# Linear attention with 64 heads: the product with the running state from unmasked queries, 16 matmuls of 144 columns in place of 64 of 36

## The chip, the cores and the metric

The kernel runs on one core of a Trainium2 chip. The metric is the device time of one execution in microseconds, the median of several runs. The core has a matrix engine (TensorE; PE in the profile, and PEld for its weight loads), a vector engine (VectorE, DVE), an activation engine (ScalarE, ACT), a general engine (GpSimd, POOL), and SyncE (SP), which here issues nearly all DMAs. Each engine runs its own list of instructions in order, and they meet at semaphores.

## The reference

The input `x` is 4 sequences of 2048 tokens of 512 features. One layer is computed: layer norm, then a causal linear attention with 64 heads of 8 features and a linear layer in fp8 values, side by side, and all of it added to `x`.

```python
xn = _layernorm(x)
q, k, v = heads(xn @ Wq.T + bq), heads(xn @ Wk.T + bk), heads(xn @ Wv.T + bv)
be = exp(beta)
q = softmax(be * q, axis=-1)          # over the 8 features of a head
k = softmax(be * k, axis=-1)
kv = cumsum(einsum('zsD,zsd->zsDd', k, v), axis=1)   # an 8x8 state per head, token by token
kn = cumsum(k, axis=1)
num = einsum('zsD,zsDd->zsd', q, kv)
den = sum(q * kn, axis=-1, keepdims=True)
attn = (num / den) @ Wo.T + bo
ffn = fp8(xn / in_scale) * in_scale @ (w_fp8 * w_scale).T + bias
out = x + attn + ffn
```

## The kernel before, in words

**Tiling.** A step takes 32 tokens (`TOK`) of each of the 4 sequences, so 128 partitions, and there are 64 steps. Heads go in groups of `J` = 4: 16 groups (`G`), each of 4 x 8 = 32 features. A value row has `VW` = 9 columns, 8 features and a one (scaled) that carries the denominator. The causal sum is split: inside a step by masked scores ("intra"), and for all earlier tokens by a running state ("inter").

**One step on TensorE** (`body(i)` of the tensor block), with the lines of the profile. Projections are 12 matmuls of 512 fp16 columns each (high and low halves of both operands). The order in a body is: keys of step i (L877 to L881 into `k_ps`); first half of the scores of step i-1 (L904) and of its state product (L921, 32x32 tiles, into `a_ps`); transposes of step i-2 (L947); queries of step i (`q_ps`); second half of scores and state; the fp8 layer of step i-2 (L979, 4 matmuls) and its output projection (L888 to L892); the **inter product** of step i-1 (L1001) into `a_ps`; values of step i (L877 to L881 into `vo_ps`); the **intra product** of step i-1 (L1020), added onto the inter product in `a_ps`. Scores, state, inter and intra are fp32. Both L1001 and L1020 use 128x32 tiles: all 128 rows of the array, and one of its four bands of 32 columns.

The inter product takes, for each of 16 groups and each of 4 heads j, the 32 tokens' queries with all but head j set to zero (`q_heads`), against a state of 4 sequences x 9 = 36 columns (`st_seqs`), and writes 32 partitions of `a_ps`, those of head j. The rows of the operands are (sequence, head in group, feature), so `st_seqs` is block-diagonal over sequences, and the zeros of `q_heads` pick the head:

```python
for g in range(G):
    for j in range(J):
        mm(a_ps[TOK * j:TOK * (j + 1), a_col(g):a_col(g) + GW],
           q_heads[:, t.parity, g, j, :], st_seqs[:, t.parity, g, :, :],
           start=(g % (G // 2) == 0), stop=False, skip_group_check=True)
```

**Around it.** VectorE masks the state product as it reads it from `a_ps` (`mask_state`, L652, two halves per step) so that only the blocks of equal heads stay. The inter product writes over the same banks, so it waits for the second of them (`masked_ready`). Then `add_state` sums the four heads' columns into `st_step` (L661) and adds that to `st_run` (L666). ScalarE spreads `st_run` over the sequences into `st_seqs` (L529, four activations of 144 columns), which the inter product of the next body reads. ScalarE also makes `q_heads` from the transposed queries `qT` (L520, four activations of 512 columns), which the scores read too, and `k_pairs` (L505).

**What sets the order.** The engines' lists are written out by hand, and each waits on semaphores only. TensorE has one list with all 62 bodies from step 2 on written out (the branch on `any_low`; the other side of it is a loop that doesn't run with these inputs). The other engines run a loop of 4 bodies. VectorE's order in a body is: `normalise_attention` of i-2, `normalise` and `quantise` of x, shift of the keys (L641, L645), masks of scores (L672), `mask_state` 0, the low half of the attention output (L749), key sums (L700 to L712), shift of the queries, masks of scores, transpose of the queries (L769), `mask_state` 1, `output` (L721), `add_state`, statistics, and in every second body `variances`, then `scale_values` (L728).

## Time and profile before

| | |
|---|---|
| runs | 1307.56, 1312.95, 1318.35 us; median 1312.95 us |
| the profiled execution | 1305.86 us; span 1304.1 us |
| mean granted clock of TensorE | 0.977 of full |
| TensorE busy | 1195.1 us, 92% of the span |
| VectorE busy | 1025.0 us, 79% |
| ScalarE busy | 661.0 us, 51% |
| GpSimd busy | 321.7 us, 25% |
| a step in the even middle part | 18.1 and 18.4 us in turn |

The busy shares are means over the span. The last row is read from the timeline, as the distance of one inter product's start to the next. Of a matmul the profile shows start and a modelled end; the ends overlap the next starts, so what a group of matmuls takes is read from its first start to the start of the group behind it. An fp32 matmul that isn't a transpose stands in the profile as two weight loads and two matmuls.

### The profile page before, as it was taken

Reading aid. Unit: us, or ns where it says so; the run is one execution under the profiler, and the core shown is the slowest. Engines: PE = TensorE matmul, PEld = TensorE weight load, DVE = VectorE, ACT = ScalarE, POOL = GpSimd, SP = SyncE. Lnnn points to the kernel's source line nnn. Section 1 sums busy time; section 2 is a strip of 40 time slices with the busy share of each in tenths; the row PEclk is TensorE's granted clock in tenths of the full one; section 3 lists DMA queues with packets and bytes.
Section 4 is the critical chain, followed back from the end, with each engine's and each line's share of the span. In section 5 each row is a group of like instructions: output and inputs, shape, how many; then the busy total and the mean of one; then the engine's idle time right before and its main releaser. Section 6 shows DMA issues by size and latency. Waiting matters only on the chain.

```text
span 1304.1 us, 72799 instructions
## 1 busy us (share of the span) xinstructions
PE 1195.1 (92%) x32226; PEld 700.8 (54%) x32226; DVE 1025.0 (79%) x2031; ACT 661.0 (51%) x1177; POOL 321.7 (25%) x590
## 2 busy tenths in 40 slices
PE   1469898889898999999999999999999999999996
PEld 1335454555455555555555555555555555555553
DVE  3668686777687788888888888888888888888873
ACT  0555454444454555555555555555555555555541
POOL 3132221221222222222222222222222222222210
PEclk8689999999999999999999999999999999999998
DMA  9024343333233334344444343334333343333321
GB/s 229 16 66 73 72 76 70 72 75 68 73 69 86 75 76 88 79 84 81 88 89 82 80 86 90 83 83 79 89 87 81 85 81 92 84 82 80 70 69 44
DMA packets 156531, 105.41 MB, mean 81 GB/s; under 512 B 111969, under 2 KB 128481, under 8 KB 156257
## 3 DMA queue, kind: packets, MB, share of 16 engines
q1 hardware_dynamic: 155536, 99.76, 35.2%
q8 instruction: 256, 4.19, 1.4%
q10 hardware_dynamic: 720, 1.31, 0.4%
q14 instruction: 19, 0.15, 0.0%
HBM read 40.20 MB, written 16.78 MB: 44 GB/s over the span
## 4 chain that ended last, share of the span: by engine, by line
PE 89%; issue 6%; DVE 2%; DMA 1%; POOL 0%; ACT 0%; SPq 0%; POOLq 0%; DVEq 0%; ACTq 0%
PE s_ps L904 10%; PE a_ps L921 7%; PE a_ps L1001 6%; PE a_ps L1020 6%; PE k_ps L877 5%; PE vo_ps L979 5%; PE vo_ps L877 5%; PE k_ps L881 4%; PE k_ps L879 4%; PE vo_ps L888 4%; PE vo_ps L890 4%; PE vo_ps L879 4%; PE vo_ps L892 4%; PE vo_ps L881 4%; PE q_ps L879 4%
## 5 line engine op out<-in xcount | busy, mean ns | idle before, releaser
L520 ACT ACTIVATE q_heads<-qT,cst 128x512 f32<-128x512 f32 x256 | 164.0, 712 | 88.1 <-DVE qT L769 88.1
L406 POOL TENSOR_TENSOR y_sum<-y,y_magic 128x512 f32<-128x512 f32 x64 | 81.5, 1273 | 433.2 <-DVE y_magic L627 433.2
L505 ACT ACTIVATE k_pairs<-kT,cst 128x512 f32<-128x512 f32 x128 | 85.4, 714 | 166.7 <-DVE kT L712 166.7
L672 DVE TENSOR_TENSOR att<-s_ps,cst 128x512 f32<-128x512 f32 x256 | 163.7, 681 | 0.4 <-PE s_ps L904 0.4
L399 POOL TENSOR_TENSOR x_split<-xn,x_split 128x512 f16<-128x512 f32 x64 | 74.1, 1158 | 318.5 <-ACT x_split L461 311.5
L904 PE MATMUL s_ps<-q_heads,k_pairs 64*64 64x128 f32 x4096 | 141.5, 276 | 0.6 <-DVE att L672 0.6
L904 PEld LDWEIGHTS s_ps<-q_heads,k_pairs 64*64 64x64 f32 x4096 | 110.6, 133 | 54.5 <-issue 54.5
L461 ACT ACTIVATE x_split<-xn 128x512 f16<-128x512 f32 x64 | 40.3, 630 | 158.6 <-DVE xn L616 158.6
L877 PE MATMUL k_ps<-w_hi,xT 128*128 128x512 f16 x256 | 100.2, 392 | 21.8 <-DMA xT<-x_split 12.1
L879 PE MATMUL vo_ps<-w_lo,xT 128*128 128x512 f16 x256 | 97.8, 382 | 4.2 <-issue 4.2
L881 PE MATMUL k_ps<-w_hi,xT 128*128 128x512 f16 x256 | 99.4, 388 | 2.3 <-issue 2.3
L1001 PEld LDWEIGHTS a_ps<-st_seqs,q_heads 128*32 128x32 f32 x8192 | 78.5, 109 | 42.0 <-issue 41.8
L881 PE MATMUL vo_ps<-w_hi,xT 128*128 128x512 f16 x256 | 97.8, 382 | 3.3 <-issue 3.3
L1020 PEld LDWEIGHTS a_ps<-v_groups,att 128*32 128x32 f32 x8192 | 77.9, 108 | 40.6 <-issue 40.5
L1020 PE MATMUL a_ps<-v_groups,att 128*32 128x36 f32 x8192 | 86.5, 200 | 14.3 <-issue 14.2
L879 PE MATMUL k_ps<-w_lo,xT 128*128 128x512 f16 x256 | 99.4, 388 | 0.0
L890 PE MATMUL vo_ps<-w_lo,ah 128*128 128x512 f16 x260 | 99.0, 381 | 0.0
L888 PE MATMUL vo_ps<-w_hi,ah 128*128 128x512 f16 x260 | 99.0, 381 | 0.0
L892 PE MATMUL vo_ps<-w_hi,al 128*128 128x512 f16 x260 | 99.0, 381 | 0.0
L1001 PE MATMUL a_ps<-st_seqs,q_heads 128*32 128x36 f32 x8192 | 85.2, 201 | 14.5 <-issue 13.3
L877 PE MATMUL vo_ps<-w_hi,xT 128*128 128x512 f16 x256 | 98.2, 384 | 0.0
L921 PE MATMUL a_ps<-vp,k_e 32*32 32x36 f32 x8064 | 97.1, 196 | 0.0
(137 smaller groups left out, 2363.8 us busy)
## 6 DMA issues: line engine op xcount, KB each, us to landing
v_groups<-vp SPq DMA_DIRECT2D x512, 36.0 KB, 3.0
x_in<-L_attn_x SPq DMA_DIRECT2D x64, 256.0 KB
x_res<-L_attn_x SPq DMA_DIRECT2D x64, 256.0 KB
out<-o_sb SPq DMA_DIRECT2D x64, 256.0 KB
w_own<-L_attn_Wk SPq DMA_DIRECT2D x1, 1024.0 KB, 13.3
w_own<-L_attn_Wq SPq DMA_DIRECT2D x1, 1024.0 KB, 15.3
w_own<-L_attn_Wv SPq DMA_DIRECT2D x1, 1024.0 KB, 17.2
att<-L_ffn_weight_fp SPq DMA_DIRECT2D x1, 1024.0 KB, 18.8
```

What stands on the lines that cost most here:

```text
L520: last = sc.activation(q_heads[:, i.parity, :, j, :], qT[:, :, :], ACT.Copy, scale=head_mask[:, j:j + 1])
L672: v.tensor_tensor(att[:, c % 2, 4 * (c // 2):4 * (c // 2) + 4, :, :] .rearrange("p g j s -> p (g j) s"), s_ps[:, DM * (c % 2):DM * (c % 2 ...
L877: mm(bank[:, :], xT[:, t.parity, 0, c, :], w_hi[:, m, c, :], start=(c == 0 and not seeded), stop=False, skip_group_check=seeded)
L879: mm(bank[:, :], xT[:, t.parity, 0, c, :], w_lo[:, m, c, :], start=False, stop=False, skip_group_check=seeded)
L881: last = mm(bank[:, :], xT[:, t.parity, 1, c, :], w_hi[:, m, c, :], start=False, stop=(c == KC - 1), skip_group_check=seeded)
L888: mm(vo_ps[:, :], ah[:, j, :], w_hi[:, MO, j, :], start=(j == 0 and not rest), stop=False, skip_group_check=rest)
L890: mm(vo_ps[:, :], ah[:, j, :], w_lo[:, MO, j, :], start=False, stop=False, skip_group_check=rest)
L892: last = mm(vo_ps[:, :], al[:, j, :], w_hi[:, MO, j, :], start=False, stop=(j == J - 1), skip_group_check=rest)
L904: last = mm(s_ps[SP * TOK * gp:SP * TOK * (gp + 1), DM * n + P * q:DM * n + P * (q + 1)], k_pairs[rows, t.parity, g, :, :].rearrange("p c ...
L921: last = mm(a_ps[rows, col:col + J * VW], k_e[rows, t.parity, TOK * g:TOK * (g + 1)], vp[rows, t.parity, v_head(g):v_head(g) + J, :], star ...
L1001: mm(a_ps[TOK * j:TOK * (j + 1), a_col(g):a_col(g) + GW], q_heads[:, t.parity, g, j, :], st_seqs[:, t.parity, g, :, :], start=(g % (G // 2 ...
L1020: last = mm(groups[TOK * j:TOK * (j + 1), n], att[:, n, q, j, :], v_groups[:, t.parity, :, n, q, j, :], start=False, stop=True, skip_group ...
```

## The change

The inter product takes the unmasked queries `qT` of a group, 32 columns, once, and a state that is block-diagonal over heads as well as sequences: 4 heads x 4 sequences x 9 = 144 columns. It writes the same 4608 columns in all per step, as 16 matmuls of 144 instead of 64 of 36. A band of 32 partitions of `a_ps` no longer holds a head of the group but a group in its quarter (u); the intra product, `wo_sorted` and `bv_sorted` follow that order. The state in `st_run` keeps its masked 4 x 9 columns per group (576 in all), so the reduction over heads goes, the addition is of 576 columns, and each of the four activations into `st_seqs` is of 576 columns. `qT` has two buffers, with other waits. To make room, `lo_abs` and `k_pairs` lie in weight buffers that are read only during setup. Lines behind the first edits shift: in the changed kernel L1001 is L999, L1020 is L1018, L904 is L900, L921 is L917, L666 is L665, L529 is L530.

```diff
-        lo_abs = sb("lo_abs", [P, KC * DM], F16)
+        lo_abs = w_own[2][:, 0:KC // 2, :].rearrange("p c d -> p (c d)").bitcast(F16)
-        qT = sb("qT", [P, G, TOK])
+        qT = sb("qT", [P, 2, G, TOK])
-        k_pairs = sb("k_pairs", [P, 2, G, SP, TOK])
+        k_pairs = w_own[1][:, :, :].rearrange("p (n c) (g s) -> p n (c g) s", n=2, s=TOK)\
+            .rearrange("p n (g c) s -> p n g c s", c=SP)
-        st_step = sb("st_step", [P, G, VW])
-        st_run = sb("st_run", [P, G, VW])
-        st_seqs = sb("st_seqs", [P, 2, G, SEQS, VW])
+        st_run = sb("st_run", [P, G, J, VW])
+        st_seqs = sb("st_seqs", [P, 2, G, J, SEQS, VW])
...
# scalar engine
                     if i.after(2):
-                        act.wait_ge(a_done, (i - 1).n)
+                        act.wait_ge(scores_done, (i - 1).n * 2)
                     for j in range(J):
-                        last = sc.activation(q_heads[:, i.parity, :, j, :], qT[:, :, :],
+                        last = sc.activation(q_heads[:, i.parity, :, j, :], qT[:, i.parity, :, :],
                                              ACT.Copy, scale=head_mask[:, j:j + 1])
...
-                        last = sc.activation(st_seqs[:, i.parity, :, b, :], st_run[:, :, :],
+                        last = sc.activation(st_seqs[:, i.parity, :, :, b, :].rearrange("p g j w -> p (g j) w"),
+                                             st_run[:, :, :, :].rearrange("p g j w -> p (g j) w"),
                                              ACT.Copy, scale=seq_mask[:, b:b + 1])
...
# vector engine
-            link(v.memset(st_run[:, :, :], 0.0))
-            link(v.memset(st_seqs[:, 0, :, :, :], 0.0))
+            link(v.memset(st_run[:, :, :, :], 0.0))
+            link(v.memset(st_seqs[:, 0].rearrange("p g j b w -> p (g j b w)"), 0.0))
...
                 dve.wait_ge(masked_ready, (t + 1).n * 2)
-                v.tensor_reduce(st_step[:, :, :], st_masked[:, :, :, :].rearrange("p g j w -> p g w j"),
-                                AX.X, ALU.add).then_inc(ststep_ready, 1)
-                dve.wait_ge(ststep_ready, (t + 1).n)
                 if t.after(1):
                     dve.wait_ge(stseqs_ready, t.n)
-                v.tensor_tensor(st_run[:, :, :], st_run[:, :, :], st_step[:, :, :], ALU.add)\
+                v.tensor_tensor(st_run[:, :, :, :], st_run[:, :, :, :], st_masked[:, :, :, :], ALU.add)\
                     .then_inc(strun_ready, 1)
...
-                    if i.after(1):
-                        dve.wait_ge(qheads_ready, i.n)
-                    v.transpose(qT[:, :, :].rearrange("p g s -> p (g s)"), q_e[:, :]).then_inc(qT_ready, 1)
+                    if i.after(2):
+                        dve.wait_ge(qheads_ready, (i - 1).n)
+                        dve.wait_ge(a_done, (i - 1).n)
+                    v.transpose(qT[:, i.parity].rearrange("p g s -> p (g s)"), q_e[:, :]).then_inc(qT_ready, 1)
...
# tensor engine
-                    pe.wait_ge(qheads_ready, (t + 1).n)
+                    pe.wait_ge(qT_ready, (t + 1).n)
...
-                    for g in range(G):
-                        for j in range(J):
-                            mm(a_ps[TOK * j:TOK * (j + 1), a_col(g):a_col(g) + GW],
-                               q_heads[:, t.parity, g, j, :], st_seqs[:, t.parity, g, :, :],
-                               start=(g % (G // 2) == 0), stop=False, skip_group_check=True)
+                    for n in range(2):
+                        for gp in range(GP):
+                            for u in range(J):
+                                g = G // 2 * n + GP * u + gp
+                                mm(a_rows[TOK * u:TOK * (u + 1), n, gp, :], qT[:, t.parity, g, :],
+                                   st_seqs[:, t.parity, g].rearrange("p j b w -> p (j b w)"),
+                                   start=(gp == 0), stop=False, skip_group_check=True)
...
-                    for q in range(G // GP):
-                        groups = a_ps[:, a_col(GP * q):a_col(GP * q) + GP * GW]\
-                            .rearrange("p (g n w) -> p n g w", g=GP, w=SP * VW)
+                    for h in range(2):
                         for n in range(SEQS // SP):
                             for j in range(J):
-                                last = mm(groups[TOK * j:TOK * (j + 1), n], att[:, n, q, j, :],
-                                          v_groups[:, t.parity, :, n, q, j, :], start=False, stop=True,
-                                          skip_group_check=True)
+                                cols = slice(GW * j + SP * VW * n, GW * j + SP * VW * (n + 1))
+                                for u in range(J):
+                                    last = mm(a_rows[TOK * u:TOK * (u + 1), h, :, cols],
+                                              att[:, n, J * h + u, j, :],
+                                              v_groups[:, t.parity, :, n, J * h + u, j, :], start=False, stop=True,
+                                              skip_group_check=True)
```

Two places in the engines' lists, as the programs were built. First TensorE, around the inter product of one body (`a_ps` is the result, `vo_ps` the bank of the projections). Before:

```order
L892 MATMUL vo_ps<-w_hi,al 128x512
L1001 MATMUL a_ps<-st_seqs,q_heads 32x36 [waits stseqs_ready,masked_ready,qheads_ready]
L1001 MATMUL a_ps<-st_seqs,q_heads 32x36 x63
L877 MATMUL vo_ps<-w_hi,xT 128x512 [waits o_ready]
L879 MATMUL vo_ps<-w_lo,xT 128x512
```

And now:

```order
L888 MATMUL vo_ps<-w_hi,al 128x512
L999 MATMUL a_ps<-st_seqs,qT 32x144 [waits stseqs_ready,masked_ready,qT_ready]
L999 MATMUL a_ps<-st_seqs,qT 32x144 x15
L873 MATMUL vo_ps<-w_hi,xT 128x512 [waits o_ready]
L875 MATMUL vo_ps<-w_lo,xT 128x512
```

Nothing changes its place; 48 fp32 matmuls, which are 192 instructions, are gone from each body. A body had 1008 weight loads and matmuls and 13 instructions that only wait or signal, 1021 in all; it has 829 now, and the list from its start to the end of the last step has 65,294 before and 53,006 now. Then VectorE, from the transpose of the queries to the statistics. Before:

```order
L769 STREAM_TRANSPOSE qT<-q_e 128x512 [waits qheads_ready,qe_ready]
L652 TENSOR_TENSOR st_masked<-a_ps,cst 128x288 [waits state_done]
L721 SCALAR_TENSOR_TENSOR o_sb<-vo_ps,out_dn,x_res 128x512 [waits stored1,r_loaded1,o_done]
L660 REGISTER_ALU
L661 TENSOR_REDUCE st_step<-st_masked 128x144 [waits masked_ready]
L666 TENSOR_TENSOR st_run<-st_run,st_step 128x144 [waits stseqs_ready,ststep_ready]
```

And now:

```order
L769 STREAM_TRANSPOSE qT<-q_e 128x512 [waits a_done,qheads_ready,qe_ready]
L654 TENSOR_TENSOR st_masked<-a_ps,cst 128x288 [waits state_done]
L720 SCALAR_TENSOR_TENSOR o_sb<-vo_ps,out_dn,x_res 128x512 [waits stored1,r_loaded1,o_done]
L662 REGISTER_ALU
L665 TENSOR_TENSOR st_run<-st_run,st_masked 128x576 [waits stseqs_ready,masked_ready]
```

One instruction fewer, and it stands behind `mask_state` 1 and `output`; ahead of them only a wait is added.

## Rows read from the trace of the kernel before

**Rows 1.** The page: busy times, and TensorE's instruction fetch (packets, MB, share).

```profile
PE 1195.1 (92%) x32226; PEld 700.8 (54%) x32226; DVE 1025.0 (79%) x2031; ACT 661.0 (51%) x1177; POOL 321.7 (25%) x590
q8 instruction: 256, 4.19, 1.4%
```

**Rows 2.** Windows, from:to length, busy (instructions) by engine, granted clock, DMA.

```profile
195.00:217.30 22.30, 20.05 (x504) 10.97 (x504) 15.60 (x33) 9.88 (x19) 5.94 (x16) 0.92 0.31 66
600.00:800.00 200.00, 198.81 (x5543) 117.11 (x5541) 171.02 (x340) 109.68 (x196) 54.85 (x105) 1.00 0.41 85
```

**Rows 3.** Timeline of TensorE, one step: start, length, what, [idle before].

```profile
706.22 1.30 PE L1001 MATMUL a_ps<-st_seqs,q_heads 128*32 128x36 f32 x128 [0.27 <-issue]
707.46 0.39 PE L877 MATMUL vo_ps<-w_hi,xT 128*128 128x512 f16 x1
...
714.09 1.10 PE L904 MATMUL s_ps<-q_heads,k_pairs 64*64 64x128 f32 x32
...
715.12 0.76 PE L921 MATMUL a_ps<-vp,k_e 32*32 32x36 f32 x64
...
715.81 0.66 PE L947 MATMUL t_ps<-cst,a_n 128*128 128x128 f32 x4
```

**Rows 4.** Timeline of VectorE and TensorE: from a state mask to the next inter product.

```profile
723.81 0.42 DVE L652 TENSOR_TENSOR st_masked<-a_ps,cst 128x288 f32<-128x288 f32 x1
...
732.37 0.69 DVE L641 TENSOR_REDUCE k_max<-k_ps 128x64 f32<-128x512 f32 x1 [0.55 <-PE k_ps L881]
...
742.25 0.42 DVE L652 TENSOR_TENSOR st_masked<-a_ps,cst 128x288 f32<-128x288 f32 x1
...
742.77 0.43 PE L1001 MATMUL a_ps<-st_seqs,q_heads 128*32 128x36 f32 x28 [0.25 <-issue]
```

**Rows 5.** Waits of TensorE put down to issue: total us, times, longest.

```profile
PE a_ps L1020 <- issue: 14.2, 10, 2.2
PE a_ps L1001 <- issue: 13.3, 29, 2.6
PE k_ps L877 <- issue: 5.3, 5, 2.3
PE vo_ps L879 <- issue: 4.2, 3, 2.1
PE vo_ps L881 <- issue: 3.3, 3, 1.6
PE k_ps L881 <- issue: 2.3, 3, 1.1
```

**Rows 6.** Timeline of TensorE at two of these stalls.

```profile
199.00 0.39 PE L879 MATMUL vo_ps<-w_lo,xT 128*128 128x512 f16 x1 [2.11 <-issue]
...
200.04 0.63 PE L881 MATMUL vo_ps<-w_hi,xT 128*128 128x512 f16 x1
...
371.00 1.30 PE L1020 MATMUL a_ps<-v_groups,att 128*32 128x36 f32 x127
374.27 0.19 PE L1020 MATMUL a_ps<-v_groups,att 128*32 128x36 f32 x1 [1.97 <-issue]
```

**Rows 7.** Groups by line, whole span: xcount, busy us, mean ns, idle before.

```profile
L661 DVE TENSOR_REDUCE st_step<-st_masked 128x144 f32<-128x576 f32 x63 | 75.2, 1193 | 0.0
L666 DVE TENSOR_TENSOR st_run<-st_run,st_step 128x144 f32<-128x144 f32 x63 | 19.4, 308 | 2.2
L672 DVE TENSOR_TENSOR att<-s_ps,cst 128x512 f32<-128x512 f32 x256 | 163.7, 681 | 0.4 <-PE s_ps L904 0.4
L520 ACT ACTIVATE q_heads<-qT,cst 128x512 f32<-128x512 f32 x256 | 164.0, 712 | 88.1 <-DVE qT L769 88.1
L529 ACT ACTIVATE st_seqs<-st_run,cst 128x144 f32<-128x144 f32 x252 | 84.7, 411 | 7.0 <-DVE st_run L666 4.0
```

**Rows 8.** Waits, as rows 5: VectorE and ScalarE behind the values.

```profile
ACT vo_ps L476 <- DVE vp L728: 97.2, 63, 5.7
...
DVE vp L728 <- PE vo_ps L881: 63.5, 63, 4.7
```

More of the change, by code:

```diff
@@ L224, in build @@
         a_view = a_halves[:, :, 0:G // 2 * GW]
+        a_rows = a_view.rearrange("p n (l r) -> p n l r", l=GP)
         setup_banks = [b[:, n * DM:(n + 1) * DM] for b, n in
@@ L260, in build @@
         scores_done, att_ready = sem("scores_done"), sem("att_ready")
-        state_done, masked_ready, ststep_ready = sem("state_done"), sem("masked_ready"), sem("ststep_ready")
+        state_done, masked_ready = sem("state_done"), sem("masked_ready")
         strun_ready, stseqs_ready = sem("strun_ready"), sem("stseqs_ready")
@@ L437, in _ @@
                     .then_inc(bias_ready, 1)
-            gp.tensor_tensor(bv_sorted.rearrange("p (j g d) -> p j g d", j=J, d=DH),
-                             bias[:, MV, :].rearrange("p (g j d) -> p j g d", j=J, d=DH),
-                             w_scale_up[:, MV:MV + 1, None, None].to_broadcast([P, J, G, DH]), ALU.mult)\
+            gp.tensor_tensor(bv_sorted.rearrange("p (u h r) -> p u h r", u=J, h=2),
+                             bias[:, MV, :].rearrange("p (h u r) -> p u h r", u=J, h=2),
+                             w_scale_up[:, MV:MV + 1, None, None].to_broadcast([P, J, 2, DM // J // 2]), ALU.mult)\
                 .then_inc(bias_ready, 1)
@@ L543, in late_weights @@
                 for oc in range(KC):
-                    last = sc.activation(wo_sorted[:, oc, :].rearrange("p (j g d) -> p j g d", j=J, d=DH),
-                                         w_nat[MO][:, oc, :].rearrange("p (g j d) -> p j g d", j=J, d=DH),
+                    last = sc.activation(wo_sorted[:, oc, :].rearrange("p (u h r) -> p u h r", u=J, h=2),
+                                         w_nat[MO][:, oc, :].rearrange("p (h u r) -> p u h r", u=J, h=2),
                                          ACT.Copy)
@@ L551, in late_weights @@
                 act.wait_ge(wl_ready, chunks - KC)
-                sc.activation(lo_abs[:, :], w_lo[:, MF, :, :].rearrange("p c d -> p (c d)"), ACT.Abs,
+                sc.activation(lo_abs, w_lo[:, MF, :, :].rearrange("p c d -> p (c d)"), ACT.Abs,
                               accum_out=lo_sum[:, :]).then_inc(lo_summed, 1)
@@ L864, in _ @@
             transpose = nc.tensor.transpose
-            def a_col(g):
-                return DM * (g // (G // 2)) + GW * (g % (G // 2))
             def v_head(g):
```

## The prediction, made before the changed kernel ran

> **What bounds the kernel now.** The page comes first: TensorE is busy for 92% of the span, VectorE for 79%, the others far less [rows 1]. In the even middle part it is 198.8 of 200 us [rows 2], so there a step is as long as what TensorE has to do, or nearly. The timeline says how nearly. The inter product starts at 742.77, and the second `mask_state` ends at 742.25 + 0.42 = 742.67; TensorE stood idle for 0.25 us and was let go by VectorE, though the row says "issue" [rows 4]. The body before it starts its inter product 0.10 us behind the mask too. So the middle part is a ring of both engines: keys done, then VectorE's list from `k_max` (732.37) to the mask's end (742.67), 10.3 us, then inter, values, intra and keys on TensorE. TensorE alone would take about 18.07 us a step, which is the distance in the last full steps; the ring takes 18.1 and 18.4 in turn. Whatever shortens the inter product shortens both.
>
> The early part is slower, 20 to 23 us a step between 195 and 400 us, and the waits of TensorE say by what: idle time that no engine released, at six lines [rows 5]. Of the 13.3 us at L1001, 7.0 are three stalls of 2.1 to 2.6 us and the rest are the small waits for the mask; of the 5.3 at k_ps L877, 0.8 lies in setup. This leaves 14.2 + 7.0 + 4.5 + 4.2 + 3.3 + 2.3 = 35.5 us. Two of them are in [rows 6]: one after the first value matmul, one before the last record of the intra product. Counted in the program's list, they are all at one place: 194 or 195 instructions behind a multiple of 256, in all of the 16 that I placed, the one at 1288 us too. The list has 65,294 instructions, 255.05 times 256, and the fetch queue moved 256 packets, 4.19 MB, so 16 KB or 256 instructions each [rows 1]. So these are fetches of instructions that come late. A body is 1021 instructions, 3 less than 4 blocks, so the boundary creeps through the body by 3 a step. It hurts while a whole block is consumed in the two dense products, where 256 instructions take 1.24 us (706.22 to 707.46 [rows 3]), and not later on. At the stall of 374.27 the block had begun with the group at 371.00: 3.3 us from block to block. With 3.45 us as the least time of a block, a count along the list gives 36.4 us of stalls against the 35.5 seen, in the same steps.
>
> The Trainium skill, Runtime: NRT & Kernel Launch, section Instruction fetch mechanics, has the 256-instruction blocks too, and says that crossing a boundary is mostly hidden, since instructions are dispatched more slowly than they are filled. By that sentence fewer instructions would be worth nothing here; the trace disagrees, with 35.5 us.
>
> **The change, part by part.**
>
> *The inter product itself.* From start to the next group's start, L1001 takes 1.24 us for 128 matmul records of 36 columns, L921 0.69 us for 64: 8.6 ns each and 0.14 us once. L904 takes 1.03 us for 32 records of 128 columns: less 0.14, 27.8 ns each [rows 3]. Four run beside each other, so one tile spends 4 x 8.6 = 34.4 ns on 36 columns and 111 on 128: 0.83 ns a column. 144 columns cost 124 ns a tile, 31.1 ns a record, and 32 records with the 0.14 make 1.13 us instead of 1.24. **This is 0.11 us a step, 64 times: 6.7 us.** The columns stay the same; only the share per instruction goes. Bounds: 0.96 us, if four tiles stream without a gap and nothing is paid once (0.28 less, -18 us); from above the overlap of tiles with 128 rows and long streams isn't in any row. L904's tiles have 64 rows. Tiles of 128 rows overlap well at 36 columns, with the same 4608 columns in 1.24 us. I take the middle value since L904 is the nearest in columns.
>
> The Trainium skill, TensorE: Matmul & The Clock Gate, section Part 3: Packing small matmuls, says that a weight load overlaps a running matmul only where the row group differs. All four tiles here have all rows, so it speaks against long streams; at 36 columns the trace disagrees, with 8.6 ns a record. The same section gives a speedup of 2.38 for three column tiles, about 0.8 of ideal; as an estimate from it the inter product would take 1.39 us, and the sum would have 10 us more in place of 6.7 less.
>
> *Instruction fetch.* A body has 192 instructions fewer, 829, which is 3 blocks and 61. The boundary jumps by 61 a step now instead of creeping by 3, and the inter product is 64 instructions instead of 256. Only a block that is nearly all intra product is consumed too fast. The same count along the new list, with 3.45 us a block, finds it in every fourth or fifth body: bodies 8, 12, 17, 21 (0.6, 1.8, 1.9, 0.7 us), 29, 33, 38, 42 (0.4, 1.6, 2.1, 0.9), 50, 54, 59, 63 (0.4, 1.6, 2.1, 0.9), and once more at the end (1.9): 17 us. It hardly depends on where the first boundary lies (15 to 18 us for any). **35.5 - 17 = 18.5 us less.** Bounds: all 35.5 gone, or none.
>
> *The clock.* After four of the eleven stalls of 1.9 us and more, six to eight matmuls came 0.43 us apart instead of 0.215 (199.66 to 202.60 is one place [rows 6]), and the granted clock of that body is 0.92 against 1.00 in the middle [rows 2]: 1.2 GHz instead of 2.4. That was 5.6 us. With four or five such stalls left, 2 to 3 us stay: **3 us less**.
>
> *VectorE.* `add_state` was 1.19 + 0.31 us; one addition of 576 columns, by the 512 of L672 at 0.68, is 0.75 [rows 7]. The 0.75 us saved lie behind `output`, outside the ring's 10.3 us, in front of a wait for the values. Costed at nothing; should the addition be dearer, the cover is VectorE's wait for the values, 63.5 us in 63 bodies, 1.0 us each [rows 8]. Without the cover each 0.1 us costs 6 us. The added wait of the transpose of the queries is for an intra product one body back: nothing.
>
> *ScalarE.* Four activations of 576 columns: by L520 at 0.71 (512) and L529 at 0.41 (144) [rows 7], some 0.75 each, 3.0 us instead of 1.4 with their overlap. Next in its queue is the seed of `vo_ps`, for which it waited 1.5 us a body [rows 8]; that takes nearly all of the added 1.5 us, and the fp8 layer on TensorE needs the seed only after scores, transposes and the query projection. `st_seqs` itself is read by the inter product a body later, about 14 us. Nothing; uncovered it would be 1.5 us a step, 96 us.
>
> *The rest.* The intra product has the same matmuls in another order: nothing. The larger memsets (2304 and 576 columns) are on VectorE at the start, ahead of a wait for the scalars' DMA: nothing, and 3 us once if that wait were shorter. The aliased buffers are free before their first new use.
>
> Sum: 6.7 + 18.5 + 3 = 28 us off the profiled execution's 1305.9, 1278. The median of the runs lies 7 above that execution, which is inside their own spread of 11; I take half: **1281 us**.
>
> **The rivals.**
>
> 1. *The fetch gain doesn't come*: the stalls stay, because late fetches follow something else in the first 500 us (the DMA load, say) and not the density of instructions. For it: they come in the first 500 us only. Against: the place modulo 256, and the one at 1288. Then 6.7 us: about 1302 to 1306. This is also how it would go by the sentence of the skill on fetching.
> 2. *The tiles overlap less*, 3.2 of them at a time: 32 x 124 / 3.2 + 0.14 us = 1.38 us for the inter product, 0.14 more a step than before. Then 9 us more where 6.7 less were counted: 1297, just faster by over 1%; 1290 to 1300 with milder forms. The section of the skill on packing would have it so. For it: L904's four tiles have half the rows. Against: the 36-column tiles.
> 3. *Slower: the bands serialise.* If a weight load or a stream of 144 columns waits for the one before, whatever the band, 32 records cost 32 x 124 ns = 4.0 us and the 0.14 once, 2.9 us more a step: 1281 + 6.7 + 185 = 1473 us. It turns the change to a loss once the inter product takes over 1.24 + 21.5 / 64 = 1.58 us, when fewer than 2.8 tiles run at a time. For it: no row shows it excluded at this length. Against: 36-column tiles of the same shape overlap almost fully.
> 4. *More*: all stalls go, and the product is at 0.96 us: 18 + 35 + 5.6 = 59 us less, 1250 to 1255.
>
> **How the numbers follow.** A difference under about 1%, 13 us, can't be told from none here. The forecast has 0.57 (its own range 1272 to 1292), rival 1 0.13, rival 2 0.18, rival 3 and weaker forms of it 0.06, rival 4 0.06. Faster by over 1%, below 1300: the forecast, rival 4 and nearly all of rival 2 are 0.79; same 0.15; slower 0.06. The range leaves out rival 3, most of rival 4 and the upper part of rival 1: 1260 to 1303.
>
> **What would show it.** In the changed profile: L999 to the next L873 in 1.1 to 1.2 us; the fetch queue with 208 packets (53,006 instructions); issue stalls of 15 to 18 us in all, in single bodies over the whole span and not in a run of bodies, mostly near L1018, and the early steps as short as the late ones; the middle steps 18.0 and 18.3 us, with the inter product still 0.1 us behind the mask. Wrong would be: an inter group over 1.5 us; more or longer stalls than 20 us; or the inter product waiting for `st_seqs`, which would mean that ScalarE's longer work isn't covered.

## The result, and the profile after

| | before | changed |
|---|---|---|
| runs, us | median 1310.48 (1307.56 to 1318.35) | median 1251.41 (1250.03 to 1252.23) |
| ratio, 95% interval | | 0.954 [0.949, 0.959] |
| the profiled execution | 1305.86 us, span 1304.1 | 1250.03 us, span 1248.2 |
| mean granted clock | 0.977 | 0.982 |
| first to last inter product | 1188.8 us | 1137.7 us |

The medians (four runs of each) are 59 us apart and the profiled executions 55.8, where the prediction's sum had 28. The forecast was 1281 us; the result lies below the predicted range of 1260 to 1303. The page of the changed kernel, for [rows 1]:

```profile
PE 1174.9 (94%) x26082; PEld 679.2 (54%) x26082; DVE 977.9 (78%) x1968; ACT 744.9 (60%) x1177; POOL 321.6 (26%) x590
q8 instruction: 209, 3.42, 1.2%
```

The fetch queue moved 209 packets where 208 were counted, 47 fewer than before. VectorE lost 47 us of work and ScalarE gained 84, and neither is seen in the time. The two windows of [rows 2], in the changed kernel:

```profile
195.00:217.30 22.30, 22.30 (x505) 13.00 (x495) 18.16 (x36) 13.11 (x21) 3.71 (x3) 1.00 0.37 90
600.00:800.00 200.00, 199.16 (x4492) 114.78 (x4490) 162.69 (x329) 125.26 (x199) 52.49 (x93) 1.00 0.38 84
```

The middle is as it was. The early window was 20.05 of 22.30 us busy at a granted clock of 0.92; now TensorE is busy without a gap at 1.00. One step's timeline of TensorE, for [rows 3], and the state mask of VectorE ahead of it, for [rows 4]:

```profile
712.25 1.19 PE L999 MATMUL a_ps<-st_seqs,qT 128*32 128x144 f32 x32
713.37 0.39 PE L873 MATMUL vo_ps<-w_hi,xT 128*128 128x512 f16 x1
...
716.07 1.31 PE L1018 MATMUL a_ps<-v_groups,att 128*32 128x36 f32 x128
```

```profile
711.73 0.42 DVE L654 TENSOR_TENSOR st_masked<-a_ps,cst 128x288 f32<-128x288 f32 x1
```

The inter product takes 1.12 us (712.25 to 713.37) and still starts 0.10 us behind the mask's end (712.15): the ring is there, with steps of 18.00 and 18.28 us in place of 18.11 and 18.40. The first nine rows of TensorE's waits, for [rows 5] and [rows 6]:

```profile
PE q_ps L1039 <- DMA w_own<-L_attn_Wk: 17.2, 1, 17.2
PE q_ps L1039 <- DVE w_lo L805: 15.0, 1, 15.0
PE k_ps L873 <- DMA xT<-x_split: 12.3, 1, 12.3
PE a_ps L999 <- issue: 5.8, 24, 0.3
PE k_ps L873 <- ACT k_ps L568: 3.8, 1, 3.8
PE k_ps L1050 <- DVE w_lo L805: 3.5, 1, 3.5
PE s_ps L1039 <- DVE w_lo L805: 3.2, 2, 2.1
PE t_ps L943 <- DVE a_n L690: 1.8, 2, 1.5
PE k_ps L873 <- issue: 0.8, 1, 0.8
```

Of the six lines of "issue" in [rows 5], the only one that is left besides the 0.8 us of setup is the inter product's, at most 0.3 us each time: the small waits for the mask. **Not one stall of instruction fetch is left.** The groups and the wait that answer to [rows 7] and [rows 8]:

```profile
L530 ACT ACTIVATE st_seqs<-st_run,cst 128x576 f32<-128x576 f32 x252 | 181.5, 797 | 0.5 <-DVE st_run L665 0.5
...
L665 DVE TENSOR_TENSOR st_run<-st_run,st_masked 128x576 f32<-128x576 f32 x63 | 47.1, 748 | 0.0
```

```profile
DVE vp L727 <- PE vo_ps L877: 86.3, 63, 2.4
```

The addition is 0.748 us (0.75 was estimated), an activation 0.80 (0.75), and VectorE's wait for the values grew from 63.5 to 86.3 us: that is where its saved work went.

**Where the 55.8 us between the profiled executions come from.** From the first inter product to the last, 51.1 us: 7.6 from 63 inter products 0.12 us shorter, 33.6 from the stalls by the profile's idle times, 4.3 from matmuls at 1.2 GHz behind them, and 5.6 that this leaves. Most of the 5.6 is a way of counting: a stall's idle time begins at the modelled end of the last matmul, 0.38 us behind its start, though the next could have come 0.215 behind it, so each of some 25 stalls cost about 0.17 us more than its row says. Behind the last inter product, 4.2 us: one stall of 1.9 and the matmuls at 1.2 GHz after it. Ahead of the first, 0.6.

### The profile page after: what moved, and what is told of

It reads as the page before. It is cut to its first block, busy times and chain, and to the rows that moved or that the text cites. A ratio compares the mean times of both kernels' runs of the same rounds, so it can differ in the third digit from the quotient of the medians.

```text
span 1248.2 us, 60447 instructions
## 1 busy us (share of the span) xinstructions
PE 1174.9 (94%) x26082; PEld 679.2 (54%) x26082; DVE 977.9 (78%) x1968; ACT 744.9 (60%) x1177; POOL 321.6 (26%) x590
## 3 DMA queue, kind: packets, MB, share of 16 engines
q8 instruction: 209, 3.42, 1.2%
## 4 chain that ended last, share of the span: by engine, by line
PE 92%; issue 3%; DVE 2%; DMA 1%; ACT 1%; POOL 1%; SPq 0%; POOLq 0%; DVEq 0%; ACTq 0%
PE s_ps L900 10%; PE a_ps L917 7%; PE a_ps L1018 6%; PE a_ps L999 6%; PE k_ps L873 5%; PE vo_ps L975 5%; PE vo_ps L873 5%; PE k_ps L877 5%; PE k_ps L875 5%; PE vo_ps L884 4%; PE vo_ps L888 4%; PE vo_ps L886 4%; PE vo_ps L877 4%; PE vo_ps L875 4%; PE q_ps L877 4%; PE q_ps L873 4%
## 5 line engine op out<-in xcount | busy, mean ns | idle before, releaser
L506 ACT ACTIVATE w_own<-kT,cst 128x512 f32<-128x512 f32 x128 | 85.5, 715 | 166.7 <-DVE kT L711 166.7
L530 ACT ACTIVATE st_seqs<-st_run,cst 128x576 f32<-128x576 f32 x252 | 181.5, 797 | 0.5 <-DVE st_run L665 0.5
L900 PE MATMUL s_ps<-q_heads,w_own 64*64 64x128 f32 x4096 | 141.3, 275 | 0.6 <-DVE att L671 0.6
L900 PEld LDWEIGHTS s_ps<-q_heads,w_own 64*64 64x64 f32 x4096 | 110.4, 132 | 54.3 <-issue 54.2
L727 DVE TENSOR_TENSOR vp<-vo_ps,vp 128x512 f32<-128x512 f32 x64 | 44.3, 692 | 86.3 <-PE vo_ps L877 86.3
L873 PE MATMUL vo_ps<-w_hi,xT 128*128 128x512 f16 x256 | 97.7, 382 | 0.0
L917 PE MATMUL a_ps<-vp,k_e 32*32 32x36 f32 x8064 | 97.6, 196 | 0.0
L873 PE MATMUL q_ps<-w_hi,xT 128*128 128x512 f16 x256 | 97.0, 379 | 0.0
L875 PE MATMUL q_ps<-w_lo,xT 128*128 128x512 f16 x256 | 97.0, 379 | 0.0
L877 PE MATMUL q_ps<-w_hi,xT 128*128 128x512 f16 x256 | 97.0, 379 | 0.0
```

Source lines behind the costliest of these rows:

```text
L506: last = sc.activation(k_pairs[:, i.parity, :, c, :], kT[:, :, :], ACT.Copy, scale=pair_mask[:, c:c + 1])
L530: last = sc.activation(st_seqs[:, i.parity, :, :, b, :].rearrange("p g j w -> p (g j) w"), st_run[:, :, :, :].rearrange("p g j w -> p (g j ...
L873: mm(bank[:, :], xT[:, t.parity, 0, c, :], w_hi[:, m, c, :], start=(c == 0 and not seeded), stop=False, skip_group_check=seeded)
L875: mm(bank[:, :], xT[:, t.parity, 0, c, :], w_lo[:, m, c, :], start=False, stop=False, skip_group_check=seeded)
L877: last = mm(bank[:, :], xT[:, t.parity, 1, c, :], w_hi[:, m, c, :], start=False, stop=(c == KC - 1), skip_group_check=seeded)
L900: last = mm(s_ps[SP * TOK * gp:SP * TOK * (gp + 1), DM * n + P * q:DM * n + P * (q + 1)], k_pairs[rows, t.parity, g, :, :].rearrange("p c ...
```

## The experiments

In all of them the two transposing DMAs (`xT`, `xq`) are plain copies of the same bytes, so that the projections' operands aren't transposed; beside that each computes what its edit says. Each is a change to one of the two kernels, and all ratios are to the kernel before. Stalls are counted here from start to start: how far apart two neighbouring matmuls are at a block's boundary, less 0.25 us, where 0.3 us or more are left. A block is 256 instructions, "the array" is the part of TensorE that runs the matmuls, and its sequencer is the part that reads the list ahead of it and waits for semaphores. In the expectations theory A is that late fetches made the difference, F that two dense blocks one behind the other are enough for a stall, E and H that a wait which holds the sequencer holds the fetch; B, C and D name other causes.

**1 and 2. Both kernels with plain copies.**

```diff
-                sp.dma_start_transpose(xT[...], x_split[...]).then_inc(x_turned, 16)
+                sp.dma_start(xT[...], x_split[...]).then_inc(x_turned, 16)
```

> The kernel before the change, but each of the two DMA transposes of a body (x_split to xT, xq_rows to xq) is a plain DMA of the same bytes, so the operands aren't transposed. This is the base of the runs that follow, which all have plain copies. Theory A (instruction fetches that start too late for two fast blocks in a row): TensorE's list and the place of the block boundaries stay, so the stalls in bodies 3 to 23 stay too, 25 to 40 us; the step on TensorE stays; 1295 to 1312. Rival D (the fetches are late because the transposes' many small packets crowd the queues): the stalls go here, 1260 to 1270.

> The changed kernel with plain copies in place of the DMA transposes. Theory A (late instruction fetches made the difference): no stalls of over 0.3 us on TensorE, 1247 to 1255, and the distance to the kernel before with copies is 50 to 62 us, as with the transposes. Rival D (the fetches are late because the transposes' many small packets crowd the queues): the distance is about 10 us.

The old kernel: 1312.8 us, ratio to the kernel before 0.999 [0.997, 1.002], with 28 stalls, 43.8 us in all. The changed one: 1248.75 us, 0.954 [0.950, 0.958], with none. The copies change nothing that can be told from none, though the DMA packets are 72,563 in place of 156,531: many small packets are not the cause. The old kernel's steps exceed 18.2 us by 55.7 us in sum, in those steps that a stall hits: a microsecond of stall costs 1.27.

**3. The changed kernel with 64 matmuls of 36 columns again**, from the same unmasked queries and the same state; with the 192 instructions a body back, all else as changed.

```diff
+                            for j in range(0, J, 1):
...
-                                   st_seqs[:, t.parity, g].rearrange("p j b w -> p (j b w)"),
+                                        st_seqs[:, t.parity, g, j:j + 1].rearrange("p j b w -> p (j b w)"),
```

> The changed kernel with plain copies, and the inter product of a body issued as 64 matmuls of 36 columns (unmasked queries, one head's columns of the block-diagonal state each) instead of 16 of 144. All edits on VectorE and ScalarE stay. A body has 1021 instructions for TensorE again, at the same places as before the change. Theory A (late instruction fetches made the difference): the stalls return in bodies 3 to 23, with the low clock behind some; the time is within 5 us of the kernel before with copies. Rival B (the gain comes from the shorter add_state on VectorE, from two buffers of qT, or from the longer streams): the stalls don't return; at most 15 us over the changed kernel with copies.

1308.64 us, 0.998 [0.995, 1.001]. The whole gain is gone, with 26 stalls back, 39.9 us. What the change did on VectorE, ScalarE, in buffers or in the order of the intra product shows no gain of its own beside the stalls.

**4. The same with 32 matmuls of 72 columns** (`range(0, J, 2)`, 64 instructions a body more than the change):

> The changed kernel with plain copies and 32 matmuls of 72 columns for the inter product, 893 instructions a body. Theory E, made from the fetch times of the runs so far: the next block is asked for when TensorE's list is read some 50 instructions behind the boundary; if a semaphore wait stands before that point the request waits too; from the end of that wait to the first instruction of the block it takes 3.4 us. From the mask to the boundary there are here 128 instructions of inter (1.1 us) and at least some of the 24 of the value projection (2.6 us) and only then intra: the block comes in time. Stalls under 2 us in all, 0 to 4 us over the changed kernel with copies (1248.75). Theory A' of the prediction (each block needs 3.45 us by itself): about 15 us over it.

1252.74 us, 0.959 [0.954, 0.963], with two stalls, 2.0 us. So halving the inter product's instructions was enough. One step's row of each, in that order:

```profile
713.28 1.30 PE L1000 MATMUL a_ps<-st_seqs,qT 128*32 128x36 f32 x128 [0.22 <-issue]
```

```profile
711.31 1.21 PE L1000 MATMUL a_ps<-st_seqs,qT 128*32 128x72 f32 x64
712.45 0.39 PE L873 MATMUL vo_ps<-w_hi,xT 128*128 128x512 f16 x1
```

With 72 columns the product takes 1.14 us: nearly all the rate is gained by 72.

**5. The old kernel with its list moved.** 352 waits for a semaphore that has long been reached, which are built as 176 instructions, stand ahead of the first body, which moves every boundary by 176 instructions and leaves the bodies as they are.

```diff
+            for _ in range(352):
+                pe.wait_ge(c_loaded, 16)
```

> The kernel before the change with plain copies, and with 176 instructions that only wait for a semaphore already reached put in at the start of TensorE's list, where it waits for weights. All later instructions move by 176 against the blocks of 256; nothing else changes. Theory A: the boundary lies where no two fast blocks follow each other in bodies 3 to 23; stalls of 2 to 8 us in all, little or no low clock; 28 to 40 us less than the same kernel without the 176. Rival C (the stalls belong to the first 400 us of the program, warm-up or the load of the queues, whatever the place of the boundary): within 5 us of it. Rival B says the same as C.

1298.35 us, 0.989 [0.984, 0.995]. The early stalls are gone (first fifteen steps 18.30 us in the mean, 21.41 without the padding), so the place in the list decides. But 14 stalls, 30.3 us, turned up between 955 and 1282 us, in bodies that had none: my count had forecast 28 to 40 us less, and 12 to 14 came. Where they sit was the way on. TensorE and VectorE at the first of them:

```profile
951.89 1.10 PE L1001 MATMUL a_ps<-st_seqs,q_heads 128*32 128x36 f32 x104 [0.27 <-issue]
955.21 0.40 PE L1001 MATMUL a_ps<-st_seqs,q_heads 128*32 128x36 f32 x24 [2.23 <-issue]
955.55 0.39 PE L877 MATMUL vo_ps<-w_hi,xT 128*128 128x512 f16 x1
955.77 0.54 PE L879 MATMUL vo_ps<-w_lo,xT 128*128 128x512 f16 x1
956.11 0.63 PE L881 MATMUL vo_ps<-w_hi,xT 128*128 128x512 f16 x1
956.54 0.63 PE L877 MATMUL vo_ps<-w_hi,xT 128*128 128x512 f16 x1
```

```profile
951.37 0.42 DVE L652 TENSOR_TENSOR st_masked<-a_ps,cst 128x288 f32<-128x288 f32 x1
```

The array had entered the block at 947.80, 4.1 us ahead of the inter product. The DMA rows have no packet of the instruction queue from 948.0 to 952.8 and one from there to 953.9; its record starts at 952.83:

```profile
q8 instruction: 1, 0.02, 5.6%
```

The mask ended at 951.79, the fetch began 1.04 us later, and the first instruction of the new block ran 2.38 us after that: 3.42 us from the mask's end. The 208 inter instructions of the old block were gone after 0.9 us. In all 13 stalled bodies of this kernel the fetch began 1.03 to 1.74 us behind the mask's end, 0.3 to 5.0 us after the block was entered; in the bodies of 37 to 62 without a stall it began 0.4 to 1.5 us after the block was entered and 2.2 to 3.1 us ahead of the mask's end. That gave the theory: **the sequencer, which asks for the next block, runs ahead of the array, stands at the wait for the mask, and asks only when the mask lets it go.** The trace has rows of the sequencer itself (PEldq) that show it standing there. L998 is its wait for the mask and the queries; the row gives how many there are, the shortest, median and longest in ns, and where they start. In this body:

```profile
L998 PEldq EVENT_SEMAPHORE  x1: 3738/3738/3738, 948.1 to 948.1; - x1
```

It came to the wait at 948.10, 3.8 us ahead of the array, and stood for 3.74 us, until 951.83, 0.04 behind the mask's end; the fetch began 0.99 us later. In the 13 stalled bodies it began 1.0 to 1.7 us behind the end of this row. The rows also show the array slowing down behind the stall: the value matmuls come 0.22, 0.34 and 0.43 us apart, where 0.215 is normal, at a granted clock of 0.52 between 955.77 and 958.50, the 1.2 GHz level.

**6 and 7. The mask ahead of the queries' transpose**, in the old kernel and in the padded one. The mask then ends up to 0.7 us earlier.

```diff
+                if t.exists() and i.exists():
+                    mask_state(t, 1)
                 if i.exists():
                     dve.wait_ge(qe_ready, (i + 1).n)
...
-                if t.exists() and i.exists():
-                    mask_state(t, 1)
```

> The kernel before the change with plain copies and VectorE's second state mask ahead of the transpose of the queries; no padding. Theory E: the stalls of bodies 2 to 6, in or just behind the inter product, go, and without a first stall the ones in intra don't follow; stalls under 8 us in all, 1255 to 1270. Rival F: the stalls of bodies 7 to 23 stay, 25 to 30 us, 1278 to 1300.

> The kernel before the change with plain copies, the 176 instructions at the start, and VectorE's second state mask ahead of the transpose of the queries. TensorE then has no wait at the inter product. Theory E: the stalls of bodies 47 to 62, which came with the wait for the mask, go: stalls under 4 us in all instead of 30, and the step falls to 18.07 us; 1255 to 1264 against 1298 without the reordering. Rival F (two fast blocks in a row, wait or not): only the shorter step, 1287 to 1291.

1285.88 us, 0.985 [0.981, 0.990], and 1282.1 us, 0.981 [0.977, 0.986]. The first lies in theory F's range, 16 us above theory E's; the second misses theory E's 1255 to 1264 by 18 us and theory F's 1287 to 1291 by 5, so neither held as it stood. The stalls stayed: 21 of them, 28.5 us, and 15, 25.1 us. I had taken it that a mask which no longer delays the array no longer delays the sequencer. It does: in the padded kernel the fetch still began 1.01 to 1.30 us behind the mask's end in every stalled body, though that end now lay 0.4 to 0.8 us ahead of the inter product, and the gaps at L1001 were 1.7 to 2.4 us in place of 2.3 to 3.0 (in both without the last body). The stall followed the mask and not the array. The sequencer's wait at L998 was only shorter, 3.01 us in the middle of its 63 times where it was 3.46 in experiment 5. Here it is for experiment 7:

```profile
L998 PEldq EVENT_SEMAPHORE  x63: 51/3011/3150, 110.3 to 1258.9; - x63
```

To take the hold away the mask must be earlier by the whole lead of the sequencer.

**8 and 9. Both masks early.** The second state mask reads the first half again and stands right behind the first, so no inter product waits for it; in the padded old kernel and in the old kernel. The state of the second half of the groups is left out by it; TensorE's list is the same.

```diff
-                dve.wait_ge(state_done, t.n * 2 + n + 1)
+                if n == 0:
+                    dve.wait_ge(state_done, t.n * 2 + 1)
...
-                    a_state[:, n, :].rearrange("p (g j w) -> p g j w", j=J, w=VW),
+                    a_state[:, 0, :].rearrange("p (g j w) -> p g j w", j=J, w=VW),
...
                         mask_state(t, 0)
+                        mask_state(t, 1)
```

> The padded old kernel (176 signals more ahead of the first body), with both state masks made early, right behind the first half of the state product; the second reads the first half again, so the state of the second half of the groups is left out. The inter product then waits for a mask that ended some 8 us before. Theory H (a fetch of instructions is asked for by TensorE's sequencer, and the sequencer stands at the wait for the mask long before the array gets there, so the fetch starts 1.0 to 1.3 us behind the mask's end, and the next block is late where 256 inter instructions follow): the stalls at L1001 in bodies 43 to 62 all go, the last bodies take 17.8 us a step in place of 19.5, one stall of about 2 us stays at the end. From the 1282.1 of the same kernel with the mask only moved ahead of the transpose (stalled steps cost 31.6 us there) this gives 1250 to 1256. Theory F (two dense blocks one behind the other are enough): the stalls stay in those bodies, 1275 to 1283.

> The old kernel with plain copies and the same two early masks (the second reads the first half again, so part of the state is left out). Theory H: the stalls of bodies 0 to 4, where the block before the boundary holds the wait, go (with the mask ahead of the transpose they were 1.6, 2.1, 1.8 and 2.2 us at 116 to 195 us). From body 5 on the boundary lies inside the inter product itself and the fetch can't be ahead there: those stalls stay in part. 1273 to 1284, against 1285.9 with the mask ahead of the transpose. Theory F: as that one, stalls of bodies 1 to 4 included, 1284 to 1289.

The padded one: 1251.47 us, 0.953 [0.949, 0.958], one stall, at the end: inside theory H's 1250 to 1256 and 24 us from F's. The sequencer's wait is gone, all 63 times (51 ns is the shortest such row):

```profile
L998 PEldq EVENT_SEMAPHORE  x63: 51/51/51, 109.7 to 1226.9; - x63
```

At the place of the rows of experiment 5 the inter product is in one piece:

```profile
945.37 1.31 PE L1001 MATMUL a_ps<-st_seqs,q_heads 128*32 128x36 f32 x128
946.62 0.39 PE L877 MATMUL vo_ps<-w_hi,xT 128*128 128x512 f16 x1
```

The old kernel, one run: 1249.83 us, where I had expected 1273 to 1284. The direction was theory H's, the size was not: I had thought that a boundary inside the inter product stalls with or without the hold. It doesn't. **The old kernel, with all its 65,294 TensorE instructions, has one stall left**, and that is 63 us less than experiment 1. The same boundary in both, with the block entered on the first matmuls of the inter product. First experiment 1, TensorE, then VectorE's mask:

```profile
288.22 1.30 PE L1001 MATMUL a_ps<-st_seqs,q_heads 128*32 128x36 f32 x128 [0.25 <-issue]
...
290.75 0.38 PE L877 MATMUL vo_ps<-w_hi,xT 128*128 128x512 f16 x1
291.90 0.39 PE L879 MATMUL vo_ps<-w_lo,xT 128*128 128x512 f16 x1 [0.77 <-issue]
```

```profile
287.70 0.42 DVE L652 TENSOR_TENSOR st_masked<-a_ps,cst 128x288 f32<-128x288 f32 x1
```

and the old kernel with early masks:

```profile
257.05 1.31 PE L1001 MATMUL a_ps<-st_seqs,q_heads 128*32 128x36 f32 x128
...
259.60 0.38 PE L877 MATMUL vo_ps<-w_hi,xT 128*128 128x512 f16 x1
259.81 0.38 PE L879 MATMUL vo_ps<-w_lo,xT 128*128 128x512 f16 x1
```

```profile
249.50 0.81 DVE L653 TENSOR_TENSOR st_masked<-a_ps,cst 128x288 f32<-128x288 f32 x2
```

The sequencer's wait in the first and in the second:

```profile
L998 PEldq EVENT_SEMAPHORE  x1: 3686/3686/3686, 284.5 to 284.5; - x1
```

```profile
L998 PEldq EVENT_SEMAPHORE  x1: 51/51/51, 253.6 to 253.6; - x1
```

In the first it ended at 288.16 and the fetch began at 289.22, 1.0 us after the inter product's start; in the second it ended at 253.68 and the fetch began at 254.76, 2.3 us ahead of the inter product, whose mask had ended at 250.31. So the fetch began 1.06 and 1.08 us behind the wait's end in the two, and only the wait had moved. In bodies 5 to 18, where the boundary lies inside the inter product, this fetch began 1.0 to 1.7 us behind the inter product's start in experiment 1 and 0.1 to 2.3 us ahead of it here. The instruction queue's rows, of 289.1 to 290.3 us in the first kernel and of 254.7 to 255.9 in the second, hold one packet each:

```profile
q8 instruction: 1, 0.02, 7.0%
```

```profile
q8 instruction: 1, 0.02, 4.9%
```

The stall that is left (1.6 us, at 1233.2) is of another kind. It lies in the last body, where no values stand between the inter and the intra product, and the sequencer had not been held; the block before it was entered at 1229.90, its successor's fetch began at 1230.72, and the array had run through the block at 1231.4 and stood until 1233.23. So two dense products one behind the other do stall without any hold, as theory F has it. It happens once, here and in experiments 1 and 3 to 8 (1.4 to 2.1 us), and not in the changed kernel.

**10 and 11. The changed kernel with the mask ahead of the transpose, and with both masks early.** The edits are those of 6 and 8.

> The changed kernel with plain copies, and with VectorE's second state mask ahead of the transpose of the queries instead of behind it. The inter product waits for that mask; it ends 0.6 us earlier. If the ring of VectorE and TensorE sets the step, both steps fall to TensorE's own 17.96 us, 0.04 and 0.32 us less: 9 to 12 us less than the changed kernel with copies. Rival: the queries' transpose and q_heads are late for the next scores, or output (0.75 us, behind the mask on VectorE) holds the values instead: 0 to 4 us less.

> The changed kernel with plain copies and the same two early masks (part of the state is left out). It has no stalls to lose. Against 1239.5 with the second mask ahead of the transpose, where a step took 17.94 us: if that is TensorE's own work, 1237 to 1241; if a ring through the mask is still in it, 1230 to 1236. Late steps of 17.6 us in both cases.

1239.47 us, 0.947 [0.943, 0.951], and 1239.66 us, 0.945 [0.941, 0.950]. The first computes all that experiment 2 does and is **9.3 us faster than it**; no kernel here was clearly faster. Steps are 17.94 and 17.95 us, and TensorE has no idle time in the middle, for [rows 2]:

```profile
600.00:800.00 200.00, 200.00 (x4616) 115.45 (x4616) 163.96 (x333) 127.34 (x202) 53.63 (x99) 1.00 0.29 84
```

So the ring cost 9 us in the changed kernel. A mask earlier still gives nothing more, because there is no stall to lose. With early masks in both, the two kernels are 10.2 us apart (experiments 9 and 11; of 9 there is one run), of which the shorter inter product makes 7.7 and the last stall 1.6: so little of the 59 us belongs to the new product itself.

**12. The changed kernel with the old reduction back on VectorE**, its result unused: 1.19 us more a step.

```diff
+                v.tensor_reduce(st_step[:, :, :], st_masked[:, :, :, :].rearrange("p g j w -> p g w j"),
+                                AX.X, ALU.add)
```

> The changed kernel with plain copies, with the old reduction over heads put back on VectorE ahead of the addition of the state (its result is not used), 1.19 us a body. My account, that add_state stands behind the ring and in front of a wait for the values: VectorE's wait for the values shrinks from 1.4 to about 0.2 us a body; 0 to 4 us over the changed kernel with copies. Rival B (the saving on VectorE counts): 10 to 75 us over it.

1255.71 us, 0.961 [0.957, 0.966], 7 us above experiment 2 and between the two expectations. No stall came. Steps are 18.19 and 18.28 us in place of 18.00 and 18.28: VectorE's wait for the values, first in experiment 2 and then here, is gone in every second body, and in those the reduction lengthens the ring.

```profile
DVE vp L727 <- PE vo_ps L877: 87.1, 63, 2.4
```

```profile
DVE vp L730 <- PE vo_ps L880: 23.8, 33, 1.6
```

The cover is about 1 us a step wide; 1.5 us of old additions fit under it, 1.94 don't.

## Why the prediction was wrong

**The inter product, 6.7 us: right.** 1.12 us was measured against the 1.13 worked out; 64 times 0.12 is 7.7. The tiles of 128 rows overlap at 144 columns as the prediction worked out. By the estimate from the Trainium skill's speedup of 2.38 for three column tiles (TensorE: Matmul & The Clock Gate, section Part 3: Packing small matmuls) it would have taken 1.39 us; the trace does not agree, with 1.12.

**Instruction fetch, 18.5 us: wrong, and this is the step that failed.** All 35.5 us went. The step took 3.45 us as the least time of a block, wherever it lies, and walked along the new list with it, which left 17 us of stalls where none came. The 3.45 itself is near what a late fetch takes: 3.42 us from the mask's end in experiment 5. What failed is that it is not a property of every block but, in all bodies but the last, of a fetch whose asking was held up. The forecast put stalls into the intra product, since a block of it is consumed in 1.24 us. But ahead of the intra product stand the twelve matmuls of the values, 2.6 us, over which the sequencer runs ahead. In the changed kernel one block was entered at 298.29 and left at 299.90, 1.6 us later, without a stall, since its fetch had begun at 297.38:

```profile
298.29 0.38 PE L875 MATMUL vo_ps<-w_lo,xT 128*128 128x512 f16 x1
298.51 0.38 PE L877 MATMUL vo_ps<-w_hi,xT 128*128 128x512 f16 x1
298.81 1.31 PE L1018 MATMUL a_ps<-v_groups,att 128*32 128x36 f32 x128
300.06 0.39 PE L873 MATMUL k_ps<-w_hi,xT 128*128 128x512 f16 x1
```

What the old kernel has and the changed one hasn't is 256 dense instructions right behind a held wait. The hold is still there: with plain copies, in 12 bodies of the changed kernel the fetch begins 1.0 to 1.5 us behind the mask. But now 64 inter instructions and 24 of the values take 3.8 us (712.25 to 716.07), more than the 3.4 that the fetch needs. With 128 (experiment 4) it is nearly always enough too, with 256 (experiment 3) not. The stalls of the old kernel in the intra product and in the keys were followers of the same hold: the fetch at the inter product is late, the next one begins only some 1.5 us (1.3 to 2.1) after the array has entered its block, and the next dense block is late too. With the hold away (experiment 9), they all went. The one of 1.9 us that was forecast for the end did not come either: in experiment 2 the fetch for it began 0.87 us ahead of the last inter product.

The Trainium skill, Runtime: NRT & Kernel Launch, section Instruction fetch mechanics, has the sequencer fetch the next page while it executes the current one. The trace agrees (a packet began 2.3 us ahead of its turn in experiment 9), and adds that a semaphore wait which holds the sequencer holds the fetch too, for the 3.74 us of the row in experiment 5, with 1.0 to 1.7 us from release to packet. The prediction used that section's sentence on dispatch only, and did not ask where the sequencer stands.

**The clock, 3 us: too small,** since it hung on the stalls that were to stay; 4.3 us and most of the 2.3 at the end came.

**VectorE and ScalarE, 0: right.** Experiment 3 has all of their changes and none of the gain. Experiment 12 shows how near the cover's end was. **The rest, 0: right.** The median counted at half its distance from the profiled execution made no difference that matters.

**The ring: right,** in that the inter product stands 0.10 us behind the mask as before. That it could be broken was not in the sum; experiment 10 gave the 9 us that it costs.

**The rivals.** Rival 4, that all stalls go, is what came, at the time it gave (1250 to 1255), with a chance of 0.06. That its time fits is in part luck: its other half, an inter product at 0.96 us, did not come, and the uncounted part of each stall and more of the clock made up for it. The forecast's walk fitted the old list because there the dense inter product stood behind the wait in every body; that it gave 36.4 us for the 35.5 seen was a test on one list only. Rivals 1, 2 and 3 fell: no stall stayed, and the inter product took 1.12 us, not 1.38 or more.

What stays open: in the padded kernels some bodies with the boundary at nearly the same distance ahead of the inter product were held and others not (in experiment 7, 61 and 58 instructions held, 55 to 46 not, 43 held again). The sequencer's rows tell most of them apart. In bodies 37 to 62 of experiments 5 and 7, no body was held whose wait at L998 began 0.37 us or more behind the array's entry into the block (22 bodies), and of the 30 where it began earlier all but three were held. Why those three were not, and what in the chip sets that time, the runs don't show. Nor do they show how close two fetches can be: in the old kernel they were never less than 3.1 us apart, in the changed one two at the end were 0.3 us apart.

## What to carry to other kernels

Stalls "by issue" at places that are a fixed number modulo the block of the list are late instruction fetches, and what made a fetch late here, in all bodies but the last, was a wait that holds the engine's sequencer ahead of a dense run of instructions. The sequencer's own rows (PEldq in the profile) show how long it stands there. Compare the time from the wait's release to the end of the dense run with the 3.4 us of a fetch: either thin out the run behind the wait (fewer, longer instructions, or slow ones between), or let the awaited work end some microseconds earlier, so that the sequencer passes before the array gets there. Before such a model is walked along a new list, move the old list by half a block and see whether the model finds the stalls again.

## What the runs showed of the hardware

- An instruction fetch is one packet of 16 KB that takes about 1 us on the queue; at a stall the first instruction of the new block ran 2.2 to 2.9 us after the packet's start, and where the sequencer had been held the packet started 1.0 to 1.7 us after the release (experiments 5 and 7).
- TensorE's sequencer came to the wait ahead of the inter product some 3.5 us before the array did, and stood there for 3.46 us in the middle of 63 times (experiments 1 and 5), 3.01 with the mask ahead of the transpose (6 and 7), and not at all with early masks (8 and 9).
- The fetch can start ahead of the array: up to 2.4 us before the array entered the block (experiment 9).
- The same 4608 columns in fp32 took 1.24 us as 128 records of 36 columns, 1.14 as 64 of 72, and 1.12 as 32 of 144.
- Stalls of 2 us cost more than their length: 55.7 us of longer steps for 43.8 us of gaps, a part of it because the matmuls behind came at 0.43 us in place of 0.215.
